# Attention over 1601 keys: wide products issued as pairs of 64-row matmuls, one key on VectorE, exponentials in three pieces

## The reference

```
q = (x @ Wq)                         # 16 heads of 64
k, v = y @ Wkv                       # y: the context, 1601 x 192
atten = softmax(q k^T / 8)           # over the 1601 keys
out = (atten @ v) @ Wproj + bproj
```

## Time and profile before

| | before |
|---|---|
| device time, median of 3 runs | 2601.31 us |
| lowest, highest | 2598.7, 2606.5 us |
| span of the profiled execution | 2605.3 us |
| TensorE busy | 2463.5 us (95%) |
| VectorE busy | 1761.7 us (68%) |
| ScalarE busy | 1201.7 us (46%) |
| GpSimd busy | 1798.6 us (69%) |

### The profile page before, as it was taken

How to read it: one execution, slowest core, us unless ns; L and a number is a source line. 1 busy time by engine, 2 the same in 40 slices (tenths; PEclk the granted TensorE clock), 3 DMA queues, 4 the chain that set the end, 5 groups by cost and what they waited for, 6 DMA issues and landing times. The chain is left out here.

```text
span 2605.3 us, 59585 instructions
## 1 busy us (share of the span) xinstructions
PE 2463.5 (95%) x23988; PEld 1541.3 (59%) x23988; DVE 1761.7 (68%) x3205; ACT 1201.7 (46%) x2037; POOL 1798.6 (69%) x1483
## 2 busy tenths in 40 slices
PE   5999999999999999999999999999987788899998
PEld 3666666666666666666666666666544122366665
DVE  5766666666666666666666666666666899766665
ACT  3343343344434334443434344343346788556665
POOL 5877777877777777777777777777511688565553
PEclk8999999999999999999999999999999899999999
DMA  7899989989999898999999999999840000021221
GB/s 207 178 183 184 185 180 174 194 173 187 179 187 179 177 193 171 187 179 185 182 188 183 177 189 178 183 183 188 172 99 1 21 1 1 14 74 55 60 59 43
DMA packets 1061619, 373.42 MB, mean 143 GB/s; under 512 B 983936, under 2 KB 1031680, under 8 KB 1061216
## 3 DMA queue, kind: packets, MB, share of 16 engines
q1 hardware_dynamic: 1061344, 369.61, 70.1%
HBM read 122.02 MB, written 4.19 MB: 48 GB/s over the span
## 5 line engine op out<-in xcount | busy, mean ns | idle before, releaser
L570 PE MATMUL psum<-yN,hT 128*128 128x384 f16 (+1 forms) x3328 | 838.2, 327 | 10.4 <-DMA lT<-xT 6.5
L571 PE MATMUL psum<-yN,lT 128*128 128x192 f16 (+1 forms) x3328 | 815.9, 246 | 0.0
L553 PE MATMUL psum<-yT,Q 128*128 128x512 f16 (+2 forms) x4096 | 744.8, 334 | 0.0
L553 PEld LDWEIGHTS psum<-yT,Q 128*128 128x128 f16 x4096 | 377.2, 97 | 374.3 <-issue 87.7
L509 POOL TENSOR_TENSOR pl<-prob,ph 128x1601 f16<-128x1601 f32 x128 | 414.3, 3237 | 222.5 <-DVE ph L852 222.5
L843 DVE TENSOR_REDUCE mx<-psum 128x1 f32<-128x801 f32 (+1 forms) x512 | 500.5, 988 | 88.9 <-PE psum L553 83.7
L509 POOL TENSOR_TENSOR xT<-xT 128x1601 f16<-128x1601 f32 x128 | 413.5, 3231 | 175.4 <-DVE xT L852 130.0
L570 PEld LDWEIGHTS psum<-yN,hT 128*128 128x128 f16 (+1 forms) x3328 | 325.7, 98 | 219.4 <-issue 13.6
L730 ACT ACTIVATE xT<-psum,nb 128x1601 f32<-128x1601 f32 x128 | 204.4, 1597 | 509.8 <-DVE nb L845 505.6
L730 ACT ACTIVATE prob<-psum,nb 128x1601 f32<-128x1601 f32 x128 | 204.4, 1597 | 508.6 <-DVE nb L845 504.4
L571 PEld LDWEIGHTS psum<-yN,lT 128*128 128x128 f16 (+1 forms) x3328 | 326.3, 98 | 6.2
(11 more groups left out here) (195 smaller groups left out, 3348.3 us busy)
## 6 DMA issues: line engine op xcount, KB each, us to landing
stage<-in_ctxN SPq DMA_DIRECT2D x96, 384.0 KB
wnat<-in_WF SPq DMA_DIRECT2D x31, 512.0 KB, 4.2
stage<-in_ctxT SPq DMA_DIRECT2D x32, 400.5 KB
stage<-in_ctxT SPq DMA_DIRECT2D x64, 200.2 KB
stage<-in_ctxT SPq DMA_DIRECT2D x32, 400.0 KB
stage<-in_ctxT SPq DMA_DIRECT2D x64, 200.0 KB
OT<-Oh SPq DMA_TRANSPOSE x256, 2.8
Q<-in_WkS SPq DMA_DIRECT2D x8, 256.0 KB, 7.6
```

Source lines behind the costliest of these rows:

```text
L553: ins = pe.matmul(psS[:, lo:hi], Q[p % 2][:, q, b, tt * P:(tt + 1) * P], yT[b][:, y, lo:hi], start=False, stop=(n == 3))
L570: pe.matmul(psO[:, 0:2 * CTX], hT[G % 2][0:k, n, :], yN[b][0:k, n, :], start=(n == 0), stop=False)
L571: ins = pe.matmul(psO[:, 0:CTX], lT[G % 2][0:k, n, :], yN[b][0:k, n, 0:CTX], start=False, stop=(n == JN - 1))
```

## The change

It is in `attention`, apart from moves of some buffers of the later layers into Q0, which grew (Q of a tile now has 6 slots in place of 4).

- Scores: nine terms (three 64-channel parts by three f16 combinations), each as two 64-row matmuls, one on partitions 0 to 63 and keys 0 to 800, one on partitions 64 to 127 and keys 800 to 1600. The two halves write different banks. The two inner banks (1024 columns) come first, then the two outer ones (289 and 288).
- Exponentials in three ACTIVATEs (inner 1024, outer 289, outer 288), each with its own sum. The next tile's inner scores wait for the first, its outer scores and the f16 copy for all.
- Sum over keys: 12 blocks of 128 keys and one of 64, as 64-row matmuls of 192 columns; each half of the partitions sums into a bank of its own. VectorE adds the two banks. Key 1600 is left to VectorE as one multiply and add.
- The f16 high copy has one buffer in place of two.
- `qk_group`: 18 matmuls of 64 rows in place of 8 of 128, and three copies on ScalarE and VectorE in place of two. Both halves of q are made in one tile, with 128-row copies.
- The context is cut into 3 + 5 pieces in place of 4 + 4; the transposed part is loaded once, not with its last 64 channels twice.

```diff
@@ sync, gpsimd: loads and cuts
-                if part < 2:
...
-                elif part < 4:
...
+                if part < 3:
+                    for n, rows in enumerate(HALVES):
+                        sp.dma_start(s[rows, :], yt[part * DK:(part + 1) * DK, 800 * n:800 * n + JH]).then_inc(done, 16)
...
-                    sp.dma_start_transpose(hT[G % 2][:, :, :], ph[G % 2]).then_inc(hi_turned[G % 2], 16)
+                    sp.dma_start_transpose(pT[G % 2][:, 0:JT, :], ph).then_inc(hi_turned[G % 2], 16)
...
-                pool.tensor_tensor(pl[G % 2][:, 0:J], prob[G % 2], ph[G % 2][:, 0:J], ALU.subtract).then_inc(lo_kept, 1)
+                pool.tensor_tensor(pl[G % 2][:, DK:P], prob[G % 2][:, JM:JE], pl[G % 2][:, 0:DK], ALU.subtract)
+                pool.tensor_tensor(pl[G % 2][:, P:], prob[G % 2][:, 0:JM], ph, ALU.subtract).then_inc(lo_kept, 1)
@@ tensor: qk_group, score, gather
+                for c in range(3):
+                    cols, keys = slice(c * P, (c + 1) * P), slice(c * DK, c * DK + P)
+                    for i, (w, q) in enumerate([(0, 0), (0, 1), (1, 0)]):
+                        for h, rows in enumerate(HALVES):
+                            ins = pe.matmul(both(n)[:, h, cols], WkD[rows, w, g, keys], qT[rows, q, g, :],
+                                            start=(i == 0), stop=(i == 2))
...
+                for pair in ((1, 2), (0, 3)):
+                    if G and pair == (0, 3):
+                        pe.wait_ge(expd_all, G)
+                    for i, (n, w, y) in enumerate(TERMS):
+                        for h, rows in enumerate(HALVES):
+                            lo, hi = CHUNKS[pair[h]]
+                            ins = pe.matmul(psS[:, lo:hi], Q[p % 2][rows, q_slot(h, n, w), b, tt * P:(tt + 1) * P],
+                                            yT[b][rows, y, n, lo - 800 * h:hi - 800 * h], start=(i == 0), stop=(i == len(TERMS) - 1))
+                    ins.then_inc(scored, 1)
...
-                    pe.wait_ge(normed, G)
+                    pe.wait_ge(o_kept, G)
...
+                for n in range(JT):
+                    for cols in (slice(0, CTX), slice(CTX, 2 * CTX)):
+                        for h, rows in enumerate(HALVES):
+                            pe.matmul(psO[h], pT[G % 2][rows, n, :], yN[b][rows, n, cols],
+                                      start=(n == 0 and cols.start == 0), stop=False)
                 pe.wait_ge(lo_turned[G % 2], 16 * (G // 2 + 1))
...
+                for n in range(JT):
+                    for h, rows in enumerate(HALVES):
+                        ins = pe.matmul(psO[h], pT[G % 2][rows, JT + 1 + n, :], yN[b][rows, n, 0:CTX],
+                                        start=False, stop=(n == JT - 1))
                 ins.then_inc(summed, 1)
@@ scalar
-                act.activation(prob[G % 2], psS, ACT.Exp, bias=nb[:, G % 2:G % 2 + 1], scale=SCALE,
-                               accum_out=den[:, G % 4:G % 4 + 1]).then_inc(expd, 1)
+                for n, cols in enumerate((INNER, OUTER[0], OUTER[1])):
+                    ins = act.activation(prob[G % 2][:, cols], psS[:, cols], ACT.Exp, bias=nb[:, G % 2:G % 2 + 1], scale=SCALE,
+                                         accum_out=den[:, G % 4, n:n + 1])
+                    if n != 1:
+                        ins.then_inc(expd if n == 0 else expd_all, 1)
...
+                act.activation(Oh[G % 2][:, 0:CTX], psU, ACT.Copy, scale=rden[:, G % 4:G % 4 + 1]).then_inc(o_hi, 1)
@@ vector
             def high(G):
-                dve.wait_ge(expd, G + 1)
+                dve.wait_ge(expd_all, G + 1)
+                dve.tensor_copy(pE[:, G % 4:G % 4 + 1], prob[G % 2][:, J - 1:J]).then_inc(p_last, 1)
                 if G >= 2:
-                    dve.wait_ge(hi_turned[G % 2], 16 * (G // 2))
-                dve.tensor_copy(ph[G % 2][:, 0:J], prob[G % 2]).then_inc(hi_kept, 1)
+                    dve.wait_ge(lo_turned[G % 2], 16 * (G // 2))
+                dve.tensor_copy(pl[G % 2][:, 0:DK], prob[G % 2][:, JM:JE])
+                if G:
+                    dve.wait_ge(hi_turned[(G - 1) % 2], 16 * ((G + 1) // 2))
+                    dve.wait_ge(lo_kept, G)
+                dve.tensor_copy(ph, prob[G % 2][:, 0:JM]).then_inc(hi_kept, 1)
...
+                dve.tensor_reduce(dsum[:, m], den[:, G % 4, :], AX_X, ALU.add).then_inc(summed_up, 1)
+                dve.wait_ge(summed_up, G + 1)
+                dve.reciprocal(rden[:, m], dsum[:, m]).then_inc(recip, 1)
+
+            def add_up(G):
+                m, be = slice(G % 4, G % 4 + 1), G // HP
+                dve.wait_ge(summed, G + 1)
+                if G % HP == 0:
+                    dve.wait_ge(row_in[be % 2], 16 * (be // 2 + 1))
+                dve.wait_ge(p_last, G + 1)
+                dve.scalar_tensor_tensor(Olo, yL[be % 2], pE[:, m], psO[1], ALU.mult, ALU.add).then_inc(olo_kept, 1)
                 dve.wait_ge(olo_kept, G + 1)
...
+                dve.tensor_tensor(psU, psO[0], Olo, ALU.add).then_inc(added_up, 1)
```

More of the change, by code:

```diff
@@ L159, in __init__ @@
         self.slots = 12
-        self.rows = full[:, 1024:].rearrange("p (n c) -> p n c", c=C)
+        self.rows = full[:, 1024:4096].rearrange("p (n c) -> p n c", c=C)
         self.hT = full[:, 0:2048]
+        self.hpre = full[:, 4096:5120].rearrange("p (n c) -> p n c", n=2)
+        self.eb1s = full[:, 5120:5632].bitcast(F16)
+        self.eb2s = full[:, 5632:5632 + C // 2].bitcast(F16)
+        self.g32 = full[:, 5760:5760 + T]
+        self.ysb = [full[:, 4096 + DI * n:4096 + DI * (n + 1)] for n in range(2)]
         self.eb2r = full[:, 1024:1024 + C]
@@ L181, in __init__ @@
         self.ident16 = half[:, 6624:6752]
+        self.cut = half[:, 8192:12288].rearrange("p (k c h n) -> p k c h n", k=KD, c=T // 8, h=2)
         self.work = full[:, 3376:3888].rearrange("p (n t) -> p n t", n=2)
@@ L457, in cut @@
                 s, N_, T_ = stage[K % RING], yN[be % 2], yT[be % 2]
-                if be == 1 and part == 4:
+                if be == 1 and part == 3:
                     pool.wait_ge(wvp_done, CUTS)
@@ L523, in q_half, with qk_group @@
                 ins.then_inc(q_done, 1)
[L525 to L531 removed]
+            def qk_group(g, n=3):
+                for c in range(3):
[4 more added lines that the diff above has]
+                                            start=(i == 0), stop=(i == 2))
                 ins.then_inc(qk_done, 1)
@@ L706, in _, with q_copy @@
         @block.scalar
         def _(act):
-            def q_copy(n, ps=psM):
+            def q_copy(n, ps):
                 half = n % 2
                 act.wait_ge(q_done, n + 1)
-                for h2 in range(2):
-                    rows = slice(DK * h2, DK * h2 + DK)
-                    ins = act.activation(qT[rows, 4 * half:4 * half + 4, h2, :], ps[rows, :].rearrange("p (g t) -> p g t", g=4),
-                                         ACT.Copy)
-                ins.then_inc(q_hi, 1)
@@ L951, in _ @@
             for g in range(4):
[L952 removed]
+                qk_low(g, KEYED[g])
             for g in range(4, HP):
@@ L1353, in state_space @@
         hs = [[sb(f"hs_{g}_{n}", [P, DI]) for n in range(2)] for g in range(NG)]
-        ysb = [sb(f"ysb{n}", [P, DI]) for n in range(2)]
+        ysb = room.ysb
         zt = Xtm[:, :, :].bitcast(F32).rearrange("p (k i) c -> p k (i c)", k=KD)
```

321 lines of the change are left out of this document (147 added, 174 removed).

## The result

| | before | after |
|---|---|---|
| device time, median of 4 runs | 2603.4 us | 2764.55 us |
| lowest, highest | 2598.7, 2606.5 us | 2762.5, 2772.32 us |
| span of the profiled execution | 2605.3 us | 2760.7 us |
| TensorE busy | 2463.5 us (95%) | 2455.0 us (89%) |
| VectorE busy | 1761.7 us (68%) | 1888.1 us (68%) |

The change makes the kernel slower: ratio 1.0628, 95% interval 1.0606 to 1.065. The spans differ by 155.4 us. The starts of the exponentials divide that. Those of tile 16 start at 180.61 us (before 165.97), of tile 240 at 1928.32 (before 1785.61), of the last tile at 2040.86 (before 1889.28). So 14.6 us come in the first pair, 128.1 us in pairs 1 to 14 (7.80 us a tile in place of 7.23, 0.57 more), 8.9 us in the last pair, and 3.8 us behind it.

A forecast was written before the change was run, and what follows sets the result against it. TensorE bounds the kernel at 7.23 us a tile; VectorE with ScalarE takes over at 7.81: +148 us. Less 3 for the start, on the 2605.3 us span: 2750; median 4 under span, short tiles 5 off: 2740, range 2660 to 2860.

The forecast's parts named there:

- signs: Profile after: TensorE under 95% busy, idle before `gather` and inner scores; VectorE's maximum no longer waiting for scores.
- (a): Exponentials in three pieces on ScalarE: 2.21 us from first start to copy, before 1.72; +0.49 us a tile.
- (b): VectorE's copies of one probability and of 64: +0.20 us a tile; main copy of 1536 columns: -0.04.
- (c): VectorE's sum of three denominators, with a wait for its end before the reciprocal: +0.18 us a tile.
- (d): End of a tile on VectorE: +0.29 us with `qk_group`; +0.86 where no `qk_low` stands between.
- (e): Third instruction of `qk_low` on VectorE: +0.34 us in a tile with `qk_group`.
- (f): VectorE's two maxima read 1024 + 578 columns in place of 801 + 800: nothing.
- GpSimd and SyncE in the steady part: GpSimd's changed cuts (busy 5.6 us a tile, under 7.8) and SyncE's changed transposes and loads cost nothing.
- Rival 1: TensorE's weight loads or pairs cost more, `gather` 4.05 us; 2850 us; chance 0.07.
- the one copy buffer: The f16 copy's wait for the previous transpose, landing 4.5 us after issue, is covered by 3 us.
- rival 3: Transpose from the one copy buffer lands after the 3 us of cover; 0.5 us a tile gives 2870; chance 0.03.
- The short tiles: VectorE's chain has tiles shorter than the pattern's in first and last pair: 5 us off.

The follow-up runs named there:

- experiment 1: Kernel after plus five unused 192-column matmuls on TensorE at the end of each `gather`: 2785.0 us, ratio 1.0699.
- experiment 2: Kernel after plus one unused 300-column reduction on VectorE behind every tile's exponentials: 2847.43 us, ratio 1.0941.
- experiment 3: Kernel after with the exponentials in one ACTIVATE with one sum, no reduction of three: 2650.13 us, ratio 1.0182.
- experiment 4: Kernel before with the exponentials in three ACTIVATEs and a reduction, everything else as it was: 2656.32 us, ratio 1.0195.
- experiment 8: Kernel after with one exponential ACTIVATE, `o_low` and `qk_low` put off into VectorE's wait for exponentials, first rest after five cuts: 2619.19 us, ratio 1.0055.
- experiment 5: Kernel after with the two banks' sum in SBUF and `o_low` moved into VectorE's wait for the exponentials: 2679.35 us, ratio 1.0284.
- experiment 9: Kernel after with one exponential ACTIVATE, only `o_low` in VectorE's wait for exponentials, first rest after five cuts: 2623.67 us, ratio 1.0082.

## Why the prediction was right, and where it missed

The forecast was 2740 us, slower, and 2764.55 lies in its range. The mechanism held: VectorE with ScalarE took over the pace, and experiments 1 and 2 show it from both sides. Of the signs, one did not come: TensorE has no idle time before the inner scores.

- **(a) exponentials:** predicted 2.21 us from the first start to the copy, measured 2.20. Experiments 3 and 4 price it as time.
- **(b), (c) small copies and sum:** 1105.68 to 1105.85 is 0.17 (predicted 0.20); the reduction adds 0.19 (predicted 0.18).
- **(d) end of a tile:** 1106.99 to 1108.75 is 1.76 without a `qk_group` (predicted 1.70). The chains came to 7.83 and 7.44 (predicted 7.92 and 7.48), the mean to 7.80 (predicted 7.81). That the mean fits so closely is in part luck: the tile that makes q takes 8.72 us, as mean of pairs 1 to 14, where 8.13 was predicted, and that makes up for most of the 0.09 us too much in eight others.
- **(e) third `qk_low`:** 1115.47 to 1116.47 for three, as predicted (3 x 0.34).
- **(f) maxima:** predicted nothing; from the first to the bias they take 1.91 us (1109.08 to 1110.99), where the tile of the earlier trace rows has 2.00 without its wait. These 0.09 us are the distance from 7.92 to 7.83.
- **GpSimd and SyncE in the steady part:** nothing, as predicted; the copy hardly waits for a transpose there.
- **Rival 1:** `gather` takes 3.06 us (predicted 3.17, the rival 4.05), `score` 3.07 (3.06; in experiment 1, where nothing stands between it and `gather`). Only `qk_group` is dearer, 0.64 us where 0.51 was predicted. Over all tiles the saving was 0.12 us of work a tile (experiment 8, with its stretches at the low clock) where I had 0.21.

What missed is the part outside the steady pace. At 0.57 us a tile 256 tiles make 146 us (predicted 148). The other 9 us of the 155.4 stand against 8 us less in the sum, its -3 and -5.

- **The start.** The sum had "First scores wait for three pieces of the cut in place of four: -3 us". They did start 3.5 us sooner (25.25, before 28.72), but tile 3's exponentials start 3.5 us later. The step that failed is that of the one copy buffer: "the next copy comes 7.5 us or more later, so it is covered by 3 us". That was read from steady tiles. At the start GpSimd's nine cuts stand ahead of the first rest, and rival 3's mechanism struck once, through GpSimd. Its wait of 7.39 us is not its price, since the kernel before waited 5.50 us for the same rest in another place; no run separates the two.
- **The short tiles.** The sum took 5 us off for shorter tiles in the first and last pair. The first pair's are longer, 9.34 us a tile (before 8.11), with the waits of the start and the statistics of line 929, which the sum left out. The last pair's are shorter, 7.50, but so are those of before, 6.91: the difference is as elsewhere. A tile that is shorter in both kernels takes nothing off.
- **Behind attention** the span grew by 3.8 us, for which the sum had nothing; no run divides it.

These are 17 us, less 2 in the steady pace: the 15 us between the +140 that the forecast amounts to and the 155.4 of the spans. The other 9 us are how the median stands to the span, 4 us above it where I had put 4 below, and rounding.

## What to carry to other kernels

A change that relieves the busiest engine is worth at most the distance to the second chain, and that chain includes its waits: VectorE was busy 67% of the time and yet had 0.45 us of slack in 6.91. Price the second chain start to start from a timeline, with the fixed cost of every instruction that splitting an operation adds (0.25 us an ACTIVATE here), before taking work off the first. And where buffers are merged, look at the first tiles by themselves: there the readers stand behind set-up work. Line up the tiles of both kernels by their place in the loop: in experiment 8 one tile of sixteen held all that was left of the loss, which the mean did not show.

## What the runs showed of the hardware

**Pairs of 64-row matmuls with new weights fit.** A group of the kernel after, 400 to 1600 us:

```profile
L578 PEld LDWEIGHTS psum<-yN,pT 64*128 64x128 f16 x7344 | 299.2, 94 | 128.2 <-DVE Oh L896 113.9 <-issue 11.6
```

75 matmuls of `gather`, each with a load of 94 ns, took 3.06 us, 41 ns each. One after another the loads would take 7.05 us, so they overlap each other and the matmuls.

**A VectorE instruction stretched beside GpSimd.** I had not expected this. In experiment 5, `o_low` reads two SBUF operands (the sum moved there) and now stands where GpSimd cuts the context. VectorE and GpSimd of one tile:

```profile
1107.77 0.28 DVE L897 SCALAR_TENSOR_TENSOR Oh<-xT,rden,Oh 128x64 f16<-128x64 f32 x1
1107.86 1.32 POOL L493 TENSOR_TENSOR yN<-stage,yN 128x576 f16<-128x576 f32 x1
...
1107.96 1.37 DVE L898 SCALAR_TENSOR_TENSOR Oh<-xT,rden,Oh 128x128 f16<-128x128 f32 x1
```

The same instruction took 341 ns with a PSUM operand (line 896 after) and 1.37 us here: it ended at 1109.33, 0.15 us after GpSimd's subtraction, which had started 0.10 us sooner (1107.86 + 1.32 = 1109.18). It is not the SBUF operand by itself. One tile earlier the same instruction started 0.08 us ahead of GpSimd's subtraction, and took 0.34 us:

```profile
1100.56 0.34 DVE L898 SCALAR_TENSOR_TENSOR Oh<-xT,rden,Oh 128x128 f16<-128x128 f32 x1
1100.64 1.82 POOL L487 TENSOR_TENSOR yT<-stage,yT 128x801 f16<-128x801 f32 x1
```

Its mean over 159 tiles is 819 ns. The Trainium skill ("SBUF — State Buffer", section "Who interferes with whom") says just this: a VectorE instruction with two SBUF inputs contends with a GpSimd instruction that reads SBUF, the lock on the shared ports is exclusive, and the order of issue decides who waits. By that rule the whole 1.32 us of GpSimd block VectorE, and the trace agrees. F32 copies between SBUF buffers are stretched beside GpSimd too: the start's copy of 1536 columns (1.50 us in the row above at 53.73, mean 953 ns) ran beside a GpSimd cast and subtraction (lines 485 and 487), and in experiment 9 one took 2.15 us beside line 487:

```profile
1110.47 1.71 POOL L487 TENSOR_TENSOR yT<-stage,yT 128x801 f16<-128x801 f32 x1
...
1110.84 2.15 DVE L874 CAST xT<-xT 128x1536 f16<-128x1536 f32 x1 [0.35 <-DMA pT<-xT]
```

So a gap in VectorE's timeline is worth less than it looks when GpSimd reads SBUF in it. In experiment 5 this one still fitted into the wait for the exponentials, of which 0.76 us were left; how much of the missing 85 us it cost was not separated.
